# A gated cross-attention and ternary-weight MLP kernel: the two weight products of each head pair with 64 moving columns per head instead of 128

## What is computed

```python
x = x + tanh(g_xattn) * xattn(layernorm(x), ctx)
x = x + tanh(g_ffn) * ffn(layernorm(x))          # three ternary-weight products, quantized activations

# xattn:
q_hk   = (hidden_q @ Wq.T).reshape(b, s, H, K)          # H=16, K=128
q_big  = einsum('bshk,hkq->bshq', q_hk, w_kc_q)         # q: 384
kv     = rope(kv_c)
q_r    = einsum('bshq,hqr->bhsr', q_big, W_qr)          # r: 64
k_r    = einsum('bld,hdr->bhlr', kv, W_kr)
attn   = softmax(einsum('bhsr,bhlr->bhsl', q_r, k_r))
ctx_c  = einsum('bhsl,bld->bhsd', attn, kv)
out    = einsum('bhsd,hkd->bshk', ctx_c, w_kc_kv).reshape(b, s, H*K) @ Wo.T
```

## Time and profile before

| what | value |
|---|---|
| median of 3 runs | 776.16 us (775.52 to 776.30) |
| the profiled execution's own time | 778.66 us |
| its span, first to last instruction | 776.8 us |
| PE busy | 729.0 us (94%), 4050 matmul instructions |
| PEld busy | 518.6 us (67%), 4050 |
| DVE busy | 584.4 us (75%) |
| ACT busy | 483.1 us (62%) |
| POOL busy | 228.9 us (29%) |
| mean granted TensorE clock | 0.982 |

### The profile page before, as it was taken

One profiled execution on the slowest core, in us unless ns is written; L12 is line 12 of the kernel. 1 busy time (PEld: TensorE's weight loads), 2 busy tenths in 40 slices (PEclk: granted clock), 3 DMA queues, 4 the chain that ended last, 5 costly groups with the idle time before them and its releaser, 6 DMA issues.

```text
span 776.8 us, 12682 instructions
## 1 busy us (share of the span) xinstructions
PE 729.0 (94%) x4050; PEld 518.6 (67%) x4050; DVE 584.4 (75%) x1008; ACT 483.1 (62%) x801; POOL 228.9 (29%) x212
## 2 busy tenths in 40 slices
PE   2789999999999999999999999999999998979996
PEld 2456777777777777777777777777777775635553
DVE  4747676777676777677888888888888897789872
ACT  2357575656565666565666666666666764558874
POOL 1412221222122222222212221322132234666641
PEclk9869999999999999999999999999999999999999
DMA  8401040104010401040113211321120001000001
GB/s 251 152 1 55 28 146 32 55 28 149 28 54 27 148 27 54 27 149 28 55 55 104 101 54 54 108 94 54 54 88 0 28 1 54 1 2 14 27 28 41
DMA packets 24977, 47.68 MB, mean 61 GB/s; under 512 B 6000, under 2 KB 11248, under 8 KB 24816
## 3 DMA queue, kind: packets, MB, share of 16 engines
q1 hardware_dynamic: 23904, 46.01, 17.5%
q10 hardware_dynamic: 976, 1.25, 0.5%
q0 software_dynamic: 64, 0.00, 0.0%
HBM read 45.16 MB, written 2.10 MB: 61 GB/s over the span
## 4 chain that ended last, share of the span: by engine, by line
PE 77%; DVE 11%; ACT 5%; issue 4%; DMA 1%; POOL 1%; DVEq 0%; ACTq 0%; SPq 0%; POOLq 0%
PE ps_b L1096 12%; PE ps_s L1042 11%; PE ps_ctx L1053 8%; PE ps_b L1016 7%; PE ps_ctx L1055 6%; PE ps_ctx L1054 6%; PE ps_s L525 6%; PE ps_b L576 4%; PE ps_b L972 4%; PE ps_b L974 4%; PE ps_b L973 4%; DVE small L1359 2%; PE ps_b L995 2%; ACT E L1208 1%; DMA x_sb<-in_x 1%
## 5 line engine op out<-in xcount | busy, mean ns | idle before, releaser
L930 POOL TENSOR_SCALAR E<-E,small 128x1024 f32<-128x1024 f32 x128 | 147.1, 1149 | 460.6 <-DVE small L1364 460.6
L1183 ACT ACTIVATE et_hi<-ps_b 128x512 fp32r<-128x512 f32 x256 | 153.1, 601 | 189.3 <-PE ps_b L1096 189.3
L1325 DVE TENSOR_TENSOR et_lo<-ps_b,et_hi 128x512 fp32r<-128x512 f32 x256 | 175.5, 686 | 56.0 <-ACT et_hi L1183 53.7
L1359 DVE TENSOR_REDUCE small<-ps_s 128x1 f32<-128x1024 f32 x128 | 155.8, 1218 | 9.6 <-PE ps_s L1042 7.9
L1096 PEld LDWEIGHTS ps_b<-ident,E 128*128 128x128 f32 x1024 | 124.8, 140 | 56.1 <-issue 16.2
L1096 PE MATMUL ps_b<-ident,E 128*128 128x128 f32 x1024 | 154.6, 274 | 7.0 <-POOL E L930 3.1
L1208 ACT ACTIVATE E<-ps_s,small 128x1024 f32<-128x1024 f32 x128 | 142.8, 1116 | 20.6 <-DVE small L1359 20.0
L1053 PE MATMUL ps_ctx<-et_hi,kv_hi 128*128 128x512 f32 x256 | 121.1, 473 | 0.2
L1055 PE MATMUL ps_ctx<-et_lo,kv_hi 128*128 128x512 f32 x256 | 101.4, 396 | 0.0
L1054 PE MATMUL ps_ctx<-et_hi,kv_lo 128*128 128x512 f32 x256 | 100.7, 394 | 0.0
L525 PE MATMUL ps_s<-wq,q12T 128*128 128x512 fp8e4 x256 | 62.0, 387 | 4.1 <-DVE h_f L769 3.7
(11 more groups left out here) (142 smaller groups left out, 1001.1 us busy)
## 6 DMA issues: line engine op xcount, KB each, us to landing
w_stage<-in_wffn SPq DMA_DIRECT2D x48, 512.0 KB, 3.5
wo_s<-in_woT SPq DMA_DIRECT2D x8, 512.0 KB, 6.0
wq_s<-in_wq SPq DMA_DIRECT2D x7, 512.0 KB, 5.7
wkcq_s<-in_wkcqT SPq DMA_DIRECT2D x7, 384.0 KB, 3.9
x_sb<-in_x SPq DMA_DIRECT2D x4, 512.0 KB, 6.7
out<-x_sb SPq DMA_DIRECT2D x8, 256.0 KB, 2.0
wqr_s<-in_wqr SPq DMA_DIRECT2D x7, 192.0 KB, 4.2
E<-in_ctx SPq DMA_DIRECT2D x2, 512.0 KB, 9.0
```

What stands on the lines that cost most here:

```text
L930: nc.gpsimd.tensor_scalar(e, e, rowinv[:, k:k + 1], 1.0, ALU.mult, ALU.mult).then_inc(scaled, 1)
L1183: return nc.scalar.activation(out, in_, ACT.Copy)
L1325: return nc.vector.tensor_tensor(out, full, hi.bitcast(F32), ALU.subtract)
L1359: nc.vector.tensor_reduce(negmax[:, k:k + 1], ps_s[:, t % 2, :], AX_X, ALU.max, negate=True).then_inc(max_done, 1)
```

## The change

Each head takes 64 moving columns in both products. "m" writes M of head h once, into columns 64h to 64h+63 of its bank. One DVE copy of 128 columns takes both to `m_sb`, 128 x 2 x 64, which stands in the place of `mz`, 128 x 2 x 128. "a" writes for each chunk and head its own 64 columns, without accumulation. The number of matmuls stays as it was, and so does the layout of `a_sb`. The memset of `mz`, its semaphore and the wait for it are gone. The buffers that are allocated behind `mz` lie 512 bytes lower in each partition.

```diff
-        mz = sa("mz", [P, 2, P])
+        m_sb = sa("m_sb", [P, 2, R])
...
-        gate_ready, mz_zeroed = sem("gate_ready"), sem("mz_zeroed")
+        gate_ready = sem("gate_ready")
...
             if kind == "m":
                 pe.wait_ge(ld_qw, 48 * q + 48)
-                if at is not None:
-                    pe.wait_ge(mz_zeroed, 1)
                 for h in range(2):
                     for t in range(QT):
-                        rhs = wqr_s[:, h, t, :].rearrange("p (o r) -> p o r", o=1).broadcast_to([P, 2, R])
-                        last = nc.tensor.matmul(into[:, h * P:(h + 1) * P].rearrange("p (o r) -> p o r", o=2),
-                                                wkcq_s[:, h, t, :], rhs, start=(t == 0), stop=(t == QT - 1))
+                        last = nc.tensor.matmul(into[:, h * R:(h + 1) * R], wkcq_s[:, h, t, :], wqr_s[:, h, t, :],
+                                                start=(t == 0), stop=(t == QT - 1))
             elif kind == "a":
 
                 pe.wait_ge(side_freed, 1 if at is not None else side_index(p, variant, ("m",)) + 1)
                 for c in range(DT):
                     for h in range(2):
-                        last = nc.tensor.matmul(into[:, c * P:(c + 1) * P], wq_s[:, h, c * P:(c + 1) * P],
-                                                mz[:, h, :], start=(h == 0), stop=(h == 1))
+                        last = nc.tensor.matmul(into[:, c * P + h * R:c * P + (h + 1) * R], wq_s[:, h, c * P:(c + 1) * P],
+                                                m_sb[:, h, :], start=True, stop=True)
...
             if kind == "m":
-                nc.vector.tensor_copy(mz[:, 0, 0:R], bank_in[:, 0:R])
-                last = nc.vector.tensor_copy(mz[:, 1, R:P], bank_in[:, P:P + R])
+                last = nc.vector.tensor_copy(m_sb[:, :, :].rearrange("p h r -> p (h r)"), bank_in[:, 0:P])
...
-            nc.vector.memset(mz[:, :, :], 0.0).then_inc(mz_zeroed, 1)
             nc.vector.memset(minus_half, -0.5)
```

## The result

The changed kernel is slower: 779.85 us, median of 6 runs (778.62 to 780.82), against 775.91 (775.21 to 778.74, 6 runs) for the kernel before on the same chip. The ratio is 1.0047, with a 95% interval of 1.0033 to 1.0061. Its profiled execution took 780.82 us, with a span of 779.0. The forecast was 774.9, with 773.0 to 776.9 as its range.

What follows compares the result with a forecast made beforehand. The prediction took PE to bound the kernel, with weight loads setting its passes. Its terms, 0.46 + 0.55 + 0.33 = 1.34 us, taken from the median of 776.16 us, gave 774.9, range 773.0 to 776.9.

Steps and rivals of the forecast that it cites:

- Rival A: In "m" and "a", columns set the pass, 53 ns off each: 9.0 us gained, 767.1 us; chance 0.06.
- rival C: In "m" and "a", load doesn't hide behind short streams, 162 ns per pass: +8.3 us, 784.5; chance 0.03.
- Term 1: Pass spacing within "m" and "a" groups falls from 112 to 109 ns: 0.46 us gained over 153 spacings.
- Term 2: Last pass of each "m" and "a" group lets the transpose go 50 ns sooner: 0.55 us over 11 groups.
- Term 3: One DVE copy of M, 280 ns, ends 65 ns sooner in five places where "a" waits: 0.33 us.
- rival D: PE's clock falls to 1.2 GHz: one more stretch costs at most 1.7 us (776.6), more is slower; chance 0.04.
- Rival B: PE's gain is waited out for DVE at the next maximum or low part: stays at 776.2 us; chance 0.12.

Runs made afterwards that it cites:

- e1: Changed kernel with the old form of both products in the prologue and pair 0 only: 776.83 us, ratio 0.9985 against the kernel before.
- e10: Changed kernel with the same 57 unread filling matmuls as e9: 773.59 us, ratio 0.9969 against the kernel before.
- e9: Kernel before with 57 unread matmuls in PE's pauses (prologue, pair 0, 13 in pair 7): 773.67 us, ratio 0.9955 against it without.
- e12: Changed kernel with the old form of both products in pair 0 alone: 776.63 us, ratio 0.9989 against the kernel before.
- e4: Changed kernel with the first product doubled as before, only the second short: 774.50 us, ratio 0.9979 against the kernel before.
- e5: Kernel before with the new form of both products in the prologue and pair 0 only: 778.66 us, ratio 1.0026 against it.
- e2: Changed kernel with M's buffer at its old size, so later addresses stay unshifted: 779.80 us, ratio 1.0033 against the kernel before.
- e7: Changed kernel with 44 unread matmuls, seven in pair 0's pauses and 37 in the prologue's: 773.18 us, ratio 0.9956 against the kernel before.
- e8: The changed kernel executed once more, unaltered: 780.43 us.
- e11: Changed kernel with the old form of both products in the prologue alone: 778.25 us, ratio 1.0022 against the kernel before.
- e3: Kernel before with only the first product at 64 columns per head, two copies kept: 778.04 us, ratio 1.0009 against it.
- e6: Changed kernel with seven unread matmuls in PE's two pauses of pair 0: 776.81 us, ratio 1.0000 against the kernel before.

## Why the prediction was wrong

- **The reading that PE bounds the kernel, and that the weights set a pass: right.** L1079, two passes of 24 columns, had shown it, and the changed passes keep their 111 to 112 ns. Rival A (columns set the pass, 0.06) and rival C (load and stream in line, 0.03) are both excluded by the same rows: passes neither at 59 nor at 162 ns.
- **Term 1, 3 ns less spacing, 0.46 us: measured zero.** I had taken the middle between 106 and 112; the upper end held. 0.106 was worked out from a length rounded to 0.01 us, too coarse for a difference of 3 ns: by the starts and ends in the same trace, unrounded, the two passes of L1079 end 111 ns apart.
- **Term 2, the last pass of a group, 50 ns each: right.** The pairs 1 to 3, with both groups in the chain, gained 0.08 to 0.09 us each on average in e1, in the changed kernel and in e10 (against e9), for 2 x 50 ns.
- **Term 3, the copy: right**, 282 ns for 280.
- **The sum therefore would have been** 0.55 + 0.33 = 0.9 us instead of 1.3. For the pairs 0 to 5 these two terms give 3 x 0.10 + 3 x 0.115 = 0.65 us, and e9 and e10 show 0.66 there; the prologue and pair 6 could not be measured by themselves.
- **The step that failed is rival D**, the clock, with a chance of 0.04 and nothing in the sum. I had its rows and named its mechanism, and argued it away with "The changed groups leave no pause in PE's stream, only shorter streams in it". I looked at pair 1, where the products stand without a pause, and not at pair 0, though the earlier trace rows show "a" waiting there. I asked whether the change makes a pause, and should have asked what it takes from PE around the pauses that are there. Its price was too low as well: I took one stretch of 3.4 us, the length of the row I had, at 1.7 us. Here it was 6.8 us in four profiles of five, at 3.0 us net. I also wrote that the clock stood low "once more" behind the prologue; the same trace has it low from 693.9 to 697.3 us too.
- **The range** allowed for one short stretch and no more, and for 0.7 us of run-to-run shift, when the kernel before itself moves between 774.2 and 780.8 us over all of its runs.
- **Rival B, given back to DVE: not seen.** The pairs 4 and 5 kept their gain, 0.10 to 0.11 us each in the changed kernel and 0.12 in e10 against e9, for 0.115 by terms 2 and 3. Pair 6 has no end that is free of the pause of pair 7.

The Trainium skill, "TensorE: Matmul & The Clock Gate", section "LDWEIGHTS (loading the stationary operand)", gave 107 ns for such a load, by which term 1 was estimated at 0.77 us. The measured spacing of 111 to 112 ns is 5 ns above it, and nothing of that term came. The same page, section "Why this matters for your kernels", names long pauses of the engine as what lets the clock fall; the traces agree only in part. In pair 0 two pauses of 0.7 and 0.8 us with streams of 64 columns around them were enough, in five profiles. In pair 7 PE pauses for 3.1 us in all twelve profiles without fills there, and the clock fell behind it in eight of them and not in four.

## What to carry to other kernels

Halving the moving columns of a matmul that brings its own 128 x 128 weights in fp32 saves one stream per group and nothing per pass: look at the spacing that a still shorter matmul of the trace has before costing it by columns. Taking work off the matmul engine cost more here than it saved, at a place where the engine already paused, since the clock fell there; read the pauses around every place that is changed, the first and the last iteration above all. Where the clock is low in a stretch with pauses, matmuls that nobody reads, in a bank that is free, are a cheap trial: with 44 of them the changed kernel, 0.47% slower without, was 0.44% (0.26 to 0.62) faster than the kernel before. But price them at each place by itself: the 13 more in pair 7 cost as much as a low stretch of 3.4 us there.

## What the runs showed of the hardware that was not expected

- The busy share of PE in the profile doesn't foretell the clock. From 58 to 61 us PE is busy 1.49 us of 3.00 before the change and 2.24 after it, and it is after it that the clock falls. Before and after:

```profile
58.00:61.00 3.00, 1.49 (x11) 1.00 0.00 0
...
58.00:61.00 3.00, 2.24 (x15) 0.83 0.00 0
```

- The kernel before runs in two groups of times: of its 25 runs beside e9 to e12, 14 lie at or under 776.4 us and 11 at 777.2 or above. What goes with it in the profiles is the clock at the pause of pair 7 before its last unit. From "m" in pair 6 to the MLP's first matmul it takes 133.0 to 133.2 us in the profiles with no low stretch there (e1, e4, e5, e12), 134.1 to 134.5 where it is 3.4 us long (before, e2, e7, e8, e11), and 135.2 to 135.5 where it is 6.8 us (the changed kernel, e3, e6). Each kernel has one or two profiles, so that this explains the two groups is argued, not shown; the mean clock of the 25 runs bears it out in part (every run at or under 776.4 us has 0.988 or more, but six of the 11 others have 0.989 too). It accounts for 2.3 us of the 4.0 by which e3's profiled execution is longer than e1's; 1.5 us more were lost before pair 0. PE alone in e3 there:

```profile
645.00:649.00 4.00, 1.77 (x10) 0.97 0.49 162
649.00:653.00 4.00, 3.13 (x16) 0.50 0.25 100
653.00:657.00 4.00, 4.00 (x17) 0.68 0.00 0
```

and in e4, which took 775.04:

```profile
645.00:649.00 4.00, 1.21 (x8) 1.00 0.70 256
649.00:653.00 4.00, 3.98 (x30) 1.00 0.00 0
653.00:657.00 4.00, 3.90 (x29) 1.00 0.00 0
```

- The low stretch of the prologue, from 31.7 to 52.2 us in the kernel before and from 36.1 to 49.8 in the changed one, was worth more than the whole change: without it, "m" of pair 0 begins 3.2 us earlier in e7 than in the changed kernel and 4.6 earlier in e9 than in the kernel before.
- Left open: whether the first product alone is enough in other executions of e3, why the second alone was not in e4, and why the stretch was half as long in e11's profile.
